# Two square roots on GpSimd by its power operation, and a convolution channel in three wide instructions

## The chip, the cores and the metric

One core of one Trainium2 chip. The metric is the device time of the whole kernel in microseconds, as the median of three runs.

## What is computed

A gated delta-rule attention layer and a mixture-of-experts layer, each added to its input and normalised. The change touches the attention only. Its reference, cut to what matters:

```python
def _short_conv(x, w):                       # 4 taps along time, one filter a channel, then silu
    xp = jnp.pad(x, ((0, 0), (cs - 1, 0), (0, 0)))
    return jax.nn.silu(sum((xp[:, i:i + t, :] * w[:, i] for i in range(cs))))
q = _short_conv(x @ Wq, conv_q)              # 8 heads of 128
k = _short_conv(x @ Wk, conv_k)              # 3 keys a token and head
v = _short_conv(x @ Wv, conv_v)              # 3 values a token and head
q = _l2norm(q) * d ** (-0.5)
k = _l2norm(k)                               # x * rsqrt(sum(x * x) + 1e-6)
def step(S, inp):                            # one token; S is 128x128 a head
    S = S * jnp.exp(gt)[..., None, None]
    for i in range(nh):
        kS = jnp.einsum('bhd,bhde->bhe', ki, S)
        S = S + bi[..., None, None] * (ki[..., None] * (vi - kS)[:, :, None, :])
    o = jnp.einsum('bhd,bhde->bhe', qt, S)
o = o * jax.lax.rsqrt(jnp.mean(o * o, -1, keepdims=True) + 1e-05) * rms_weight
o = o * jax.nn.silu(gate)
```

x is 2 x 2048 x 256.

## The kernel before

**Stages.** A setup splits the input and the weights into 16-bit pairs and makes small tables; then comes the recurrence over blocks, then the experts. The recurrence has 128 blocks: 8 stretches of 256 tokens for each of 16 pairs of batch and head. A block is cut into 8 chunks of 32 tokens, whose 96 keys and 32 queries make 128 rows; within a chunk the delta rule is a triangular system, inverted level by level (`level_x`, `level_t`, `level_tt`), and the state is carried from chunk to chunk (`from_state`, `solve`, `update`).

**Order.** The five engines run the same written-out pipeline. `run_bodies` calls each engine's `body(k)` 135 times; in body i, `k[s]` is the block i - s, so that up to 8 blocks are in work, and every engine does its instructions in the order of its `body`, each after its semaphore waits. `done(engine, count, key, n)` waits until the instruction `key` of block n has been done. The labels of stages differ between engines: GpSimd's `k[0]` is the block that ScalarE calls `k[1]`.

**The keys' norm.** GpSimd squares the keys (`square`, L1300), TensorE sums them (`norms`, L681), VectorE adds epsilon (`small_sq`, L1115: `k_sq`, 8 columns). ScalarE takes the root of `k_sq` as Exp(0.5 Ln(x)) in `key_ln` (L959) and `key_root` (L964); the result `sv` scales the values in VectorE's `keep_v` (L1160).

**The outputs' norm.** ScalarE sums the squares of the outputs (`square_outputs`), VectorE joins them with the queries' norms (`sum_squares`, L1200: `v_sum`, 2 columns), ScalarE takes the reciprocal root in `var_ln` (L1012) and `var_root` (L1018), and GpSimd scales the outputs by it (`scale_outputs`, L1340: `o_norm`). TensorE transposes `o_norm` (`turn_outputs`, L819), and VectorE multiplies by the gate (`gated_outputs`, L1208: `y_buf`), which SP stores. Ln and Exp lie in another table of ScalarE than Silu; it is loaded ahead of `var_ln` (L1063) and changed back at the next `silu` (L942). `exp_decay` (L954) lies between and needs it as well.

**The decay and the system.** TensorE makes the decays' exponents (`decays`, L717), ScalarE exponentiates them (`decay_tok`), GpSimd spreads them (`spread_decay`, L1291). TensorE makes the gram products (`gram`, L691), VectorE scales them by the decays (`system`, L1136: `n_t`), GpSimd subtracts the identity in place (`minus_one`, L1327), ScalarE rounds (`high`, L969), VectorE masks (`first_level`, L1145), TensorE transposes (`turn_first`, L725), and GpSimd makes the rest of the rounding (`low`, L1334: `n_low`).

**The convolution.** Seven channels of a block are convolved: six by ScalarE and VectorE from PSUM (L920, L1109), one, channel 6, by GpSimd from a copy in SBUF (`raw`, L928). GpSimd's is `tap(6, i, k)`: a scale by the filter's tap 0 (L1315), and for each of three more taps a scale into `tap_now` (L1319) and an add into `pool_acc` (L1321), on 256 columns each.

GpSimd's order in a body before:

```python
tap(6, 2, k[1]); scale_outputs(k[4]); piece(k[3]); tap(6, 3, k[1]); low(1, k[1])
square(k[0]); g_rows(k[0]); spread_decay(0, k[0]); spread_decay(1, k[0])
minus_one(0, k[0]); minus_one(1, k[0]); tap(6, 0, k[0]); tap(6, 1, k[0]); low(0, k[0]); square_q(k[1])
```

`piece` (L1352, L1354) splits a piece of the experts' weights, in 96 of the passes.

## Time and profile before

| | us |
|---|---|
| median of three runs | 4454.95 |
| the three runs | 4454.95, 4439.0, 4459.3 |
| span of the profiled execution | 4438.1 |
| TensorE matmul busy in it | 3992.3 (90%) |
| VectorE busy | 3484.2 (79%) |
| ScalarE busy | 3346.6 (75%) |
| GpSimd busy | 2391.0 (54%) |

In the rows PE is TensorE, DVE is VectorE, ACT is ScalarE, POOL is GpSimd and SPq is SyncE's DMA issue; L1340 is a line of the kernel. A wait's arrow points to what released it. Matmuls overlap and their ends are modelled. A share over the whole span mixes the setup, the recurrence and the experts, so waits and timelines of the recurrence are read beside it.

### The profile page before, as it was taken

The numbers are of one execution on the slowest core, as the hardware profiler recorded it, in microseconds if no ns is written. First come the engines' busy times: TensorE is split into PE (matmuls) and PEld (weight loads), VectorE is DVE, ScalarE is ACT, GpSimd is POOL, SyncE is SP. The second block draws the span as 40 slices with busy tenths as digits, with TensorE's granted clock in tenths as the row PEclk, the third lists the DMA queues.
The fourth block names the chain that finished last, engine by engine and source line by source line (L and its number), as shares of the span: only waits on it lengthen the run. The fifth ranks groups of instructions, "written<-read, shape, count | busy, mean of one in ns | idle before, by whom it ended". The sixth has DMA issues, their size and how long they took to land. (4 is left out here: it accounts for less than half of the span.)

```text
span 4438.1 us, 131600 instructions
## 1 busy us (share of the span) xinstructions
PE 3992.3 (90%) x47876; PEld 3643.0 (82%) x47876; DVE 3484.2 (79%) x9803; ACT 3346.6 (75%) x9029; POOL 2391.0 (54%) x2511
## 2 busy tenths in 40 slices
PE   1999999999999999999999999999999665899991
PEld 0899889899988888989889899998998454788881
DVE  6899999999998888999999999999998222444446
ACT  2888888888888888888888888888888211555551
POOL 3667666766765666676666666676667023000005
PEclk6999999999999999999999999999999887899996
DMA  6223223323333333332333333233332232666664
GB/s 255 59 83 104 77 77 90 100 73 83 104 83 72 83 85 83 86 90 85 82 90 87 85 89 86 85 92 85 83 86 80 87 117 89 221 228 232 232 235 129
DMA packets 307823, 485.07 MB, mean 109 GB/s; under 512 B 38784, under 2 KB 252800, under 8 KB 288384
## 3 DMA queue, kind: packets, MB, share of 16 engines
q1 hardware_dynamic: 290448, 449.65, 34.4%
q0 software_dynamic: 6144, 16.79, 1.2%
q10 hardware_dynamic: 10608, 10.23, 0.7%
q8 instruction: 404, 6.62, 0.6%
q14 instruction: 219, 1.79, 0.1%
HBM read 352.02 MB, written 107.75 MB: 104 GB/s over the span
## 5 line engine op out<-in xcount | busy, mean ns | idle before, releaser
L1109 DVE SCALAR_TENSOR_TENSOR conv_acc<-bank,conv_sb,conv_acc 128x256 f32<-128x256 f32 x2304 | 1090.0, 478 | 14.1 <-ACT conv_acc L920 4.7
L669 PE MATMUL bank<-x_cur,w_cur 128*128 128x259 f16 (+1 forms) x6144 | 856.1, 275 | 27.9 <-DVE v_rows L1097 24.9
L1168 DVE CAST_PREDICATED xs_lev<-mask_sb,bank 128x256 f16<-128x256 uint16 x1536 | 663.1, 432 | 96.8 <-PE bank L733 74.1
L980 ACT ACTIVATE inv<-bank 128x256 f16<-128x256 f32 x1536 | 606.5, 395 | 73.8 <-PE bank L745 53.0
L669 PEld LDWEIGHTS bank<-x_cur,w_cur 128*128 128x128 f16 (+1 forms) x6144 | 565.0, 98 | 92.9 <-DVE v_rows L1097 25.8
L1291 POOL TENSOR_TENSOR decay<-decay_tok,cst 128x512 f32<-128x512 f32 x256 | 320.1, 1272 | 489.2 <-ACT decay_tok L954 489.2
L989 ACT ACTIVATE invt<-bank 128x256 f16<-128x256 f32 x1280 | 509.0, 398 | 90.4 <-PE bank L757 71.6
L788 PE MATMUL bank<-state,kq_t 128*128 128x128 f32 x2048 | 447.9, 301 | 2.0 <-DVE state L1191 2.0
L733 PE MATMUL bank<-inv,n_high 128*128 128x64 f16 x6144 | 431.7, 192 | 3.8 <-issue 1.2
L796 PE MATMUL bank<-rhs,inv_t 128*128 128x128 f32 x2048 | 427.8, 301 | 3.1 <-DVE rhs L1184 3.1
L803 PE MATMUL bank<-w_sol,k_rows 128*128 128x128 f32 x2048 | 422.4, 298 | 2.1 <-ACT w_sol L999 1.9
L1327 POOL TENSOR_TENSOR n_t<-n_t,cst 128x512 f32<-128x512 f32 x256 | 326.5, 1275 | 172.8 <-DVE n_t L1136 172.7
L1300 POOL TENSOR_TENSOR squares<-kq_t 128x768 f32<-128x768 f32 x128 | 187.8, 1467 | 398.9 <-ACT kq_t L942 398.9
L920 ACT ACTIVATE conv_acc<-bank,conv_sb 128x256 f32<-128x256 f32 x768 | 364.2, 474 | 23.7 <-PE bank L669 4.6
L1191 DVE SCALAR_TENSOR_TENSOR state<-state,tables,bank 128x128 f32<-128x128 f32 x1024 | 339.8, 342 | 40.3 <-PE bank L803 21.2
L999 ACT ACTIVATE w_sol<-bank 128x128 f32<-128x128 f32 x1024 | 280.8, 275 | 111.9 <-PE bank L796 111.7
L745 PE MATMUL bank<-xs_lev,invt 128*128 128x64 f16 x5120 | 360.3, 192 | 2.2 <-ACT inv L980 0.4
L1319 POOL TENSOR_SCALAR tap_now<-raw_in,conv_sb 128x256 f32<-128x256 f32 x384 | 355.5, 926 | 12.3
L1184 DVE SCALAR_TENSOR_TENSOR rhs<-bank,tables,v_rows 128x128 f32<-128x128 f32 x1024 | 353.3, 345 | 10.5 <-PE bank L788 6.8
L757 PE MATMUL bank<-invt,xs_lev 128*128 128x64 f16 x5120 | 360.0, 192 | 1.4 <-issue 0.3
L1136 DVE SCALAR_TENSOR_TENSOR n_t<-bank,c_n,decay 128x128 f32<-128x128 f32 x1024 | 288.5, 345 | 85.6 <-PE bank L691 73.0
L1932 POOL DMA_INDIRECT y_one<-y_slots,y_row x32 | 30.3, 948 | 589.0 <-PEq L1925 579.6
(245 smaller groups left out, 11501.8 us busy)
## 6 DMA issues: line engine op xcount, KB each, us to landing
w_cur<-w_parts_scratch SPq DMA_DIRECT2D x128, 1024.0 KB, 10.5
ew<-e_parts_scratch SPq DMA_DIRECT2D x117, 896.0 KB, 6.2
x_cur<-x_parts_scratch SPq DMA_DIRECT2D x128, 259.0 KB, 7.2
x_slots<-no_rows SPq DMA_DIRECT2D x128, 256.0 KB, 10.4
e_parts_scratch<-e_pair SPq DMA_DIRECT2D x96, 224.0 KB, 7.4
o_rows<-w_sol SPq DMA_DIRECT2D x512, 32.0 KB, 4.0
y_scratch<-y_buf SPq DMA_DIRECT2D x128, 128.0 KB, 10.1
y_in<-y_scratch SPq DMA_DIRECT2D x32, 512.0 KB, 4.0
```

What stands on the lines that cost most here:

```text
L669: last = mm(bank[i % 2][:, 0:PW], w_cur[k.i % 2][:, wp, kt, c * P:(c + 1) * P].bitcast(BF16 if wp else F16), x_cur[k.i % 2][:, xp, kt, 0:P ...
L733: last = mm(packed(LEVX[:, u * HP:(u + 1) * HP], l), n_high[k.i % 2][g][:, u], half(inv[k.i % R_LEV][g][:, u], l, 0), start=True, stop=True)
L745: last = mm(packed(LEVT[:, u * HP:(u + 1) * HP], l), by[:, u], half(xs_lev[g][l - 1][:, u], l, 0), start=True, stop=True)
L757: last = mm(packed(LEVTT[:, u * HP:(u + 1) * HP], l), xs_lev[g][l - 1][:, u], half(invt[k.i % R_LEV][g][:, u], l, 1), start=True, stop=True)
L788: mm(chain(k), kq_t[k.i % R_KQ][:, c].rearrange("p a b -> p (a b)"), state[:, k.i % (B * H)], start=True, stop=True).then_inc(ks_made.sem, 1)
L796: mm(chain(k), inv_t[k.i % R_INV][:, c], rhs[k.i % 2][:], start=True, stop=True).then_inc(sol_made.sem, 1)
L803: mm(chain(k), k_rows[k.i % R_ROWS][:, c], w_sol[k.i % R_W][:, c], start=True, stop=True).then_inc(upd_made.sem, 1)
L920: a(conv_acc[turn_of(c, k, ON_DVE, 2)][:], bank[i % 2][:, 0:TB], ACT.Copy, scale=conv_sb[:, k.h, c, 0:1])\
L980: a(half(inv[k.i % R_LEV][g][:], l, 0), packed(halves(LEVT), l), ACT.Copy).then_inc(t_kept.sem, 1)
L989: a(half(dst, l, 1), packed(halves(LEVTT), l), ACT.Copy).then_inc(tt_kept.sem, 1)
L1109: v.scalar_tensor_tensor(acc, bank[at % 2][:, i:i + TB], conv_sb[:, k.h, c, i:i + 1], acc, ALU.mult, ALU.add).then_inc(tap_step.sem if i < ...
L1168: v.copy_predicated(half(xs_lev[g][l - 1][:], l, 0), half(mask4(l), l, 0).bitcast(U16), packed(halves(LEVX), l)).then_inc(x_kept.sem, 1)
```

## The change

ScalarE's four small activations for the roots go. GpSimd computes `sv` as `k_sq` to the power 0.5 in one instruction (`key_root`, between `spread_decay(1)` and `minus_one(0)`), and `rstd` in two (`var_root`, at the head of its body ahead of `scale_outputs`): an addition of epsilon and the power -0.5; a constant factor moves into `neg_rms`. Its convolution becomes `convolve`: one product of the four overlapping windows with the four taps (1024 columns), an add of the two halves (512 columns), and an add of what is left (256 columns), all behind `minus_one(1)`. To make room in SBUF, three constant tables that only the setup uses get a buffer of their own that is given up after the setup, so that the constants come by three DMAs in place of one. `sum_squares` now waits for the previous `rstd`, and `small_sq` for the `sv` of two blocks before. GpSimd's body after begins `var_root(k[4])`, `scale_outputs(k[4])`, `piece(k[3])`, `low(1, k[1])`, and the rest keeps its order but for `key_root(k[0])` and `convolve(6, k[0])`.

```diff
-C_ID, C_NEG, C_LATER, C_UPTO, C_ONES, C_SAME = range(6)
+C_ID, C_ONES, C_SAME = range(3)
+C_NEG, C_LATER, C_UPTO = range(3)
...
-        cst = sb("cst", [P, 6, P], F32)
+        cst = sb("cst", [P, 3, P], F32)
...
             scope = setup_scope
+            cst_once = sb("cst_once", [P, 3, P], F32)
...
                     sp.dma_start(wz_stage[:].rearrange("p a b -> p (a b)"), w_z).then_inc(z_in, 16)
-                    sp.dma_start(cst[:].rearrange("p a b -> p (a b)"), consts[:, 0:6 * P]).then_inc(consts_in, 16)
+                    sp.dma_start(cst[:, 0], consts[:, 0:P]).then_inc(consts_in, 16)
+                    sp.dma_start(cst_once[:].rearrange("p a b -> p (a b)"), consts[:, P:4 * P]).then_inc(consts_in, 16)
+                    sp.dma_start(cst[:, 1:3].rearrange("p a b -> p (a b)"), consts[:, 4 * P:6 * P]).then_inc(consts_in, 16)
...
                     nc.scalar.activation(alog_sb[:], alog_sb[:], ACT.Exp).then_inc(ac, 1)
-                    nc.scalar.activation(neg_rms[:], rms_raw[:], ACT.Copy, scale=-1.0)
+                    nc.scalar.activation(neg_rms[:], rms_raw[:], ACT.Copy, scale=-((EPS_RMS * DH) ** -0.5))
...
                                         ALU.subtract).then_inc(x_split_b, 1)
-                    dve.wait_ge(consts_in, 32)
+                    dve.wait_ge(consts_in, 64)
...
                     v.tensor_copy(identb[:], cst[:, C_ID])
-                    v.tensor_copy(negmask[:], cst[:, C_NEG, 0:CH])
-                    v.tensor_copy(laterb[:], cst[:, C_LATER])
-                    v.tensor_copy(uptob[:], cst[:, C_UPTO])
+                    v.tensor_copy(negmask[:], cst_once[:, C_NEG, 0:CH])
+                    v.tensor_copy(laterb[:], cst_once[:, C_LATER])
+                    v.tensor_copy(uptob[:], cst_once[:, C_UPTO])
...
             pool_acc = ring("pool_acc", R_PACC, [P, TB], F32)
-            tap_now = sb("tap_now", [P, TB], F32)
-            scaled_tap = sem("scaled_tap")
+            tap_prod = sb("tap_prod", [P, TAPS, TB], F32)
+            windows_scaled, taps_halved = sem("windows_scaled"), sem("taps_halved")
...
             c_k = ring("c_k", 2, [P, UN], F32)
-            ln_k = sb("ln_k", [P, UN], F32)
...
             v_sum = sb("v_sum", [P, 2], F32)
-            ln_v = sb("ln_v", [P, 2], F32)
             rstd = sb("rstd", [P, 2], F32)
+            v_eps = sb("v_eps", [P, 2], F32)
+            powers = sb("powers", [P, 2], F32)
             o_norm = sb("o_norm", [P, 2, P], F32)
-            eps_var = sb("eps_var", [P, 1], F32)
...
             squared, q_squared, g_made, scaled = map(sem, ("squared", "q_squared", "g_made", "scaled"))
-            gate_done, ln_made, norm_made, o_squared, var_ln_made, rstd_made = map(sem, (
-                "gate_done", "ln_made", "norm_made", "o_squared", "var_ln_made", "rstd_made"))
+            gate_done, norm_made, o_squared, var_made, rstd_made, powers_set = map(sem, (
+                "gate_done", "norm_made", "o_squared", "var_made", "rstd_made", "powers_set"))
...
                 (6, 1),))
-            pool_step = Count("pool_step", (
-                ((6, 2), 1), ((6, 0), 0), ((6, 1), 0)))
             pool_tapped = Count("pool_tapped", (
-                (6, 1),))
+                (6, 0),))
...
                     @at_stage
-                    def key_ln(k):
-                        done(act, rows_kept, "norms", k.n)
-                        a(ln_k[:], k_sq[k.i % 2][:], ACT.Ln).then_inc(ln_made, 1)
-
-                    @at_stage
-                    def key_root(k):
-                        act.wait_ge(ln_made, k.n + 1)
-                        a(sv[k.i % 2][:], ln_k[:], ACT.Exp, scale=0.5).then_inc(norm_made, 1)
-
-                    @at_stage
...
                         last.then_inc(o_squared, 1)
-
-                    @at_stage
-                    def var_ln(k):
-                        done(act, rows_kept, "queries", k.n)
-                        a(ln_v[:], v_sum[:], ACT.Ln, bias=eps_var[:, 0:1], scale=EPS_RMS * DH).then_inc(var_ln_made, 1)
-
-                    @at_stage
-                    def var_root(k):
-                        act.wait_ge(var_ln_made, k.n + 1)
-                        at_least(act, scaled, k.n)
-                        a(rstd[:], ln_v[:], ACT.Exp, scale=-0.5).then_inc(rstd_made, 1)
...
                         nc.scalar.preload_act_table_set("natural_log_exp_and_others")
-                        var_ln(k[4])
...
                         keep_t(5, 1, k[2])
-                        key_ln(k[1])
                         raw(6, k[1])
-                        key_root(k[1])
...
                         keep_w(6, k[3])
-                        var_root(k[4])
...
                     v.memset(state[:], 0.0)
-                    v.memset(eps_var[:], EPS_RMS * DH * EPS_K)
...
                         done(dve, rows_made, "norms", k.n)
+                        at_least(dve, norm_made, k.n - 1)
...
                         dve.wait_ge(o_squared, k.n + 1)
-                        at_least(dve, var_ln_made, k.n)
+                        at_least(dve, rstd_made, k.n)
...
                     @at_stage
-                    def tap(c, i, k):
-                        acc, src = pool_acc[turn_of(c, k, ON_POOL, R_PACC)][:], raw_in[turn_of(c, k, ON_POOL, R_RAW)][:, i:i + TB]
-                        if i == 0:
-                            done(pool, silu_done, *before(c, k, ON_POOL, R_PACC))
-                            done(pool, raw_kept, c, k.n)
-                            nc.gpsimd.tensor_scalar(acc, src, conv_sb[:, k.h, c, 0:1], None, ALU.mult).then_inc(pool_step.sem, 1)
-                            return
-                        at = TAPS * len(ON_POOL) * k.n + TAPS * ON_POOL.index(c) + i
-                        done(pool, pool_step, (c, i - 1), k.n)
-                        nc.gpsimd.tensor_scalar(tap_now[:], src, conv_sb[:, k.h, c, i:i + 1], None, ALU.mult).then_inc(scaled_tap, 1)
-                        pool.wait_ge(scaled_tap, at - at // TAPS)
-                        tt(acc, tap_now[:], acc, ALU.add).then_inc(pool_step.sem if i < TAPS - 1 else pool_tapped.sem, 1)
+                    def convolve(c, k):
+                        raw = raw_in[turn_of(c, k, ON_POOL, R_RAW)][:]
+                        windows = bass.AP(raw.tensor, raw.offset, [raw.ap[0], [1, TAPS], [1, TB]])
+                        done(pool, raw_kept, c, k.n)
+                        tt(tap_prod[:], windows, conv_sb[:, k.h, c, :, None].broadcast_to([P, TAPS, TB]), ALU.mult)\
+                            .then_inc(windows_scaled, 1)
+                        pool.wait_ge(windows_scaled, k.n + 1)
+                        tt(tap_prod[:, 0:2], tap_prod[:, 0:2], tap_prod[:, 2:4], ALU.add).then_inc(taps_halved, 1)
+                        done(pool, silu_done, *before(c, k, ON_POOL, R_PACC))
+                        pool.wait_ge(taps_halved, k.n + 1)
+                        tt(pool_acc[turn_of(c, k, ON_POOL, R_PACC)][:], tap_prod[:, 0], tap_prod[:, 1], ALU.add)\
+                            .then_inc(pool_tapped.sem, 1)
+
+                    @at_stage
+                    def key_root(k):
+                        done(pool, rows_kept, "norms", k.n)
+                        done(pool, rows_kept, ("values", 1), k.n - 2)
+                        tt(sv[k.i % 2][:], k_sq[k.i % 2][:], powers[:, 0:1].broadcast_to([P, UN]), ALU.pow).then_inc(norm_made, 1)
+
+                    @at_stage
+                    def var_root(k):
+                        done(pool, rows_kept, "queries", k.n)
+                        nc.gpsimd.tensor_scalar(v_eps[:], v_sum[:], EPS_K, None, ALU.add).then_inc(var_made, 1)
+                        pool.wait_ge(var_made, k.n + 1)
+                        tt(rstd[:], v_eps[:], powers[:, 1:2].broadcast_to([P, 2]), ALU.pow).then_inc(rstd_made, 1)
...
                     def body(k):
-                        tap(6, 2, k[1])
+                        var_root(k[4])
...
                         piece(k[3])
-                        tap(6, 3, k[1])
...
                         spread_decay(1, k[0])
+                        key_root(k[0])
...
                         minus_one(1, k[0])
-                        tap(6, 0, k[0])
-                        tap(6, 1, k[0])
+                        convolve(6, k[0])
...
+                    nc.gpsimd.memset(powers[:, 0:1], 0.5).then_inc(powers_set, 1)
+                    nc.gpsimd.memset(powers[:, 1:2], -0.5).then_inc(powers_set, 1)
+                    pool.wait_ge(powers_set, 2)
```

## Rows read from the trace of the kernel before

**Rows 1.** The page: busy time, share of the span and instructions of each engine.

```profile
PE 3992.3 (90%) x47876; PEld 3643.0 (82%) x47876; DVE 3484.2 (79%) x9803; ACT 3346.6 (75%) x9029; POOL 2391.0 (54%) x2511
```

**Rows 2.** Stretches: length, each engine's busy time (instructions), granted clock, DMA share, GB/s.

```profile
2000.00:3000.00 1000.00, 971.67 (x12685) 902.92 (x12685) 914.90 (x2635) 885.49 (x2475) 678.24 (x721) 1.00 0.31 88
```

**Rows 3.** Waits of TensorE over the recurrence: total us, times, longest.

```profile
PE bank L819 <- POOL o_norm L1340: 68.6, 124, 4.2
...
PE bank L699 <- DVE y_buf L1208: 21.0, 26, 2.2
```

**Rows 4.** Waits of GpSimd, VectorE, ScalarE over the recurrence, as rows 3.

```profile
POOL decay L1291 <- ACT decay_tok L954: 489.2, 128, 5.1
POOL squares L1300 <- ACT kq_t L942: 398.9, 128, 21.9
...
DVE y_buf L1208 <- DMA y_scratch<-y_buf: 45.7, 56, 2.6
...
ACT decay_tok L954 <- PE bank L717: 73.7, 128, 2.3
```

**Rows 5.** Timeline of GpSimd, one pass: start us, us, line, operation, idle before.

```profile
2007.96 1.27 POOL L1327 TENSOR_TENSOR n_t<-n_t,cst 128x512 f32<-128x512 f32 x1 [0.18 <-DVE n_t L1136]
2010.40 1.28 POOL L1327 TENSOR_TENSOR n_t<-n_t,cst 128x512 f32<-128x512 f32 x1 [1.17 <-DVE n_t L1136]
2011.65 0.93 POOL L1315 TENSOR_SCALAR pool_acc<-raw_in,conv_sb 128x256 f32<-128x256 f32 x1
2012.67 0.92 POOL L1319 TENSOR_SCALAR tap_now<-raw_in,conv_sb 128x256 f32<-128x256 f32 x1
...
2014.37 1.16 POOL L1334 TENSOR_TENSOR n_low<-n_t,n_high 128x512 bf16<-128x512 f32 x1
2015.48 0.61 POOL L1307 TENSOR_TENSOR q_sq<-kq_t 128x256 f32<-128x256 f32 x1
...
2017.08 0.73 POOL L1321 TENSOR_TENSOR pool_acc<-tap_now,pool_acc 128x256 f32<-128x256 f32 x1
2017.77 0.61 POOL L1340 TENSOR_TENSOR o_norm<-o_rows,rstd 128x256 f32<-128x256 f32 x1
...
2043.37 0.61 POOL L1340 TENSOR_TENSOR o_norm<-o_rows,rstd 128x256 f32<-128x256 f32 x1
```

**Rows 6.** Timelines of TensorE and VectorE, same pass, as rows 5.

```profile
2008.02 1.13 PE L691 MATMUL bank<-kq_t 128*128 128x128 f32 x8
...
2018.43 0.44 PE L819 MATMUL bank<-cst,o_norm 128*128 128x128 f32 x2 [0.53 <-POOL o_norm L1340]
...
2009.19 1.13 DVE L1136 SCALAR_TENSOR_TENSOR n_t<-bank,c_n,decay 128x128 f32<-128x128 f32 x4 [0.48 <-PE bank L691]
```

**Rows 7.** Groups of ScalarE by line: busy us, mean ns, idle before.

```profile
L1063 ACT ACT_TABLE_LOAD x133 | 170.6, 1283 | 22.6 <-DVE v_rows L1097 20.4
```

**Rows 8.** Groups of GpSimd by line and shape, columns as in rows 7.

```profile
L1300 POOL TENSOR_TENSOR squares<-kq_t 128x768 f32<-128x768 f32 x128 | 187.8, 1467 | 398.9 <-ACT kq_t L942 398.9
...
L1352 POOL CAST e_pair<-e_raw 128x448 f16<-128x448 f32 x96 | 53.6, 558 | 0.0
...
L1472 POOL CAST idx<-topi 128x8 f32<-128x8 uint32 x1 | 0.2, 191 | 0.1
...
L1469 POOL MEMSET eps_ln<- 128x1 f32 x1 | 0.1, 100 | 3.6 <-POOLq L585 3.6
```

**Rows 9.** VectorE's timeline, and lines L227, L1145: duration ns min/median/max, first and last start.

```profile
25.86 4.09 DVE L305 CAST ident<-cst 128x128 f16<-128x128 f32 x1
...
L227 POOL TENSOR_TENSOR w_pair<-w_stage,w_pair x8: 4055/4058/7137, 22.7 to 92.9; 128x2048 bf16<-128x2048 f32 x8
...
2013.30 0.28 DVE L1145 TENSOR_TENSOR first<-n_high,mask_sb 128x256 f16<-128x256 f16 x1
...
L1145 DVE TENSOR_TENSOR first<-n_high,mask_sb x256: 277/282/294, 131.2 to 3432.2; 128x256 f16<-128x256 f16 x128
```

**Rows 10.** Timeline of SyncE's DMA issues in the setup, columns as in rows 5.

```profile
1.64 0.43 SPq L200 DMA_DIRECT2D cst<-in_consts  x1
```

## The prediction

> **What bounds the kernel now.** The recurrence is 135 passes of one loop body, one in 25.6 us (from one `o_norm` to the next) [rows 5]; around it lie a setup and the experts, which the change hardly touches. I read the views in this order. The shares of the span put TensorE first with 90% [rows 1], and a stretch of 1000 us in the middle of the recurrence shows what that means there: TensorE is busy for 97% at the full granted clock (2.4 GHz), VectorE for 91%, ScalarE for 89%, GpSimd for 68% [rows 2]. So a faster engine other than TensorE is worth something only where TensorE waits for it. TensorE's waits name one such place that comes back in nearly every pass: the transposes of the scaled outputs (L819) wait for GpSimd's `o_norm`, 68.6 us in 124 times. The only other repeated one is 21.0 us in 26 times at L699, behind VectorE's `y_buf` [rows 3].
>
> Next, what makes `o_norm` late. GpSimd's long waits, for `decay_tok` and for the keys, come earlier in its round [rows 4], so its queue has caught up there, and what counts is the piece from the last wait to `o_norm`. In the timeline of one pass the second `n_t` starts at 2010.40 us after 1.17 us of idleness, and from its end on the queue runs without a pause, through five of the seven convolution instructions, `n_low` and `q_sq`, to `o_norm` at 2017.77 us [rows 5]. That `n_t` was released by VectorE's at 2009.19 us, and this by TensorE's gram product of 2008.02 us; TensorE has been waiting for 0.53 us when L819 starts at 2018.43 us [rows 6]. So a loop is closed each pass: gram product, `system(1)`, GpSimd's queue, `o_norm`, transposes. A tenth of a microsecond put into GpSimd's queue between `minus_one(1)` and `scale_outputs` is paid 128 times; a tenth taken out is gained 128 times, until the 68.6 us are used up.
>
> **The change, part by part.** *ScalarE loses four small activations a pass* (`var_ln`, `key_ln`, `key_root`, `var_root`). The table load ahead of them (1.28 us) stays, since `exp_decay` needs it [rows 7], and so does the one back at the next `silu`. TensorE has no repeated wait for ScalarE [rows 3], and `decay_tok`, for which GpSimd waits, itself waits for TensorE [rows 4]. I take nothing for it: TensorE's instructions cover it.
>
> *The root for the keys* goes between `spread_decay(1)` and `minus_one(0)`. Its input comes from `small_sq`, which VectorE does ahead of `system(0)`, so it waits for nothing. Behind it stand the first `n_t`, with 0.18 us of idleness ahead of it, and the second, with 1.17 us [rows 5]: up to 1.35 us never reach the second `n_t`. It delays the first, for which ScalarE (`high(0)`) and through it TensorE (`turn_first(0)`) wait; that lies between the gram product and L819, where a small delay only uses up part of TensorE's wait at L819. Nothing, then, while a power of 8 values is under 1.35 us; beyond that every further tenth is on the loop.
>
> *The convolution.* The starts give 2017.77 - 2011.65 = 6.12 us from the first scale to `o_norm`; 1.11 of it are `n_low`'s and 0.59 `q_sq`'s, so 4.42 are convolution [rows 5]. After, all of the convolution stands there: a product of 1024 columns, an add of 512, one of 256. For the product I take the line through `o_norm` (256 columns, 0.61 us, also with a broadcast operand) and `n_low` (512, 1.16 us), 2.14 ns a column: 1.16 + 512 x 0.00214 = 2.25 us [rows 5]. From above the line through the instructions that write in place, 0.73 and 1.27 us: 2.35. From below the squaring, 768 columns in 1.47 us [rows 8], 1.67 ns a column over the 0.61: 1.89. The add of 512 is in place like `n_t`, 1.27 us (from below 1.04, by the squaring's price); the last add lies between 0.61 and 0.73, and I take 0.67. A dependent instruction starts 0.09 us after the end of its forerunner (2011.65 + 0.93 to 2012.67), an independent one 0.03 us ahead of it [rows 5]. Sum 2.25 + 0.09 + 1.27 + 0.09 + 0.67 - 0.03 = 4.34 us against 4.42. The four slow scales go, but the last scale and add, which stood behind `o_norm`, have come ahead of it: a draw on the loop, whatever GpSimd's busy time falls by.
>
> *The root for the outputs* has the price. It comes directly ahead of `scale_outputs`: an addition on 2 columns, a gap, the power on 2 columns, a gap. Its input is ready (`sum_squares` ran in the pass before); the new wait of `sum_squares` for its result has most of a pass of slack. For the addition the nearest row is the cast of 8 columns, 0.19 us; from below the memset's 0.10. From above 0.71: a scale of 256 columns lasts 0.93 us [rows 5], and the two casts (448 columns 0.56, 8 columns 0.19) [rows 8] give 0.8 ns a column, so that up to 0.7 of the 0.93 may be fixed. The power shows nowhere in the trace. From below the memset's 0.10 us, from above, for the range, the 0.93 us of the dearest instruction of 256 columns; I take 0.30 us, near the small rows, for it has 2 columns only, and above the cast, for a power is more than a cast. With gaps 0.19 + 0.09 + 0.30 + 0.09 = 0.67 us.
>
> *Sum.* 4.34 + 1.11 + 0.59 + 0.67 = 6.71 us against 6.12: `o_norm` comes 0.59 us later, over 128 passes 75.5 us. Off it goes what other waits give back: where VectorE waits for the store of `y_buf` [rows 4], the store lands when it did, so each of the 26 waits at L699 (0.81 us in the mean) shrinks by up to 0.59 us, 15 us at most; as some are shorter I take 13. Net +62 us.
>
> *The rest.* Behind `o_norm` GpSimd has 1.7 us less to do, but what follows there is again a wait for ScalarE's keys [rows 4]: more idleness, nothing else. In the setup SP issues two more DMAs, each 0.43 us [rows 10], of the same bytes; between nothing and 0.9 us, and I take nothing, since VectorE and GpSimd are behind it with their wide subtractions.
>
> **A rule of the skill against the trace.** In the setup the two engines shut each other out: VectorE's cast of 128 columns took 4.09 us beside GpSimd's wide subtractions, and the longest of these 7.1 us where the median is 4.06 [rows 9]. In the recurrence VectorE's only long instruction with two operands in SBUF is `first_level` (L1145). The one at 2013.30 us ran inside a GpSimd scale (2012.67 to 2013.59, [rows 5]) and lasted 0.28 us; none of the 256 took over 0.294 [rows 9]. The Trainium skill (SBUF — State Buffer, section on the two separate sides) says that such a VectorE instruction and a GpSimd instruction that reads SBUF exclude each other for their whole length. The setup agrees, the recurrence does not. By that rule the wide product would hold `first_level(1)` back for some 0.6 us and GpSimd's add would then wait; this is case 5.
>
> **The cases.** (1) *Forecast*: the two operations ahead of `o_norm` are paid in each pass, 4517 us. For it: the wait at L819 comes in nearly all passes, so no slack takes them up. (2) *Faster, the other side*: the wide instructions run at the squaring's price. Then product 1.89, adds 1.04 and 0.61, roots and gaps 0.38 to 0.50: 5.77 to 5.9 us, `o_norm` 0.22 to 0.35 us sooner, 28 to 45 us less, 4410 to 4427. It decides from where product, adds, root and gaps together fall below 4.42 us (5.01 in my sum). Against it: the squaring reads one tensor twice, the product two. (3) *No change*: cheap small operations and a product near 2.1 us, 6.0 to 6.3 us in all, 4440 to 4475. (4) *The power is a long routine*: at 1.0 us for 2 columns 0.7 x 128 = 90 us above the forecast, 4607; at 3 us for each root, the keys' 1.65 beyond its cover, (2.7 + 1.65) x 128 = 557 above it, 5074. Nothing in the trace speaks for or against. (5) *Exclusion*: GpSimd's add waits some 0.25 us for a `first_level` that was itself held back (0.28 us from the product's end, less the 0.09 gap that is there anyway): 26 us more, 4543. (6) *It does not do what it says*: the keys' root isn't hidden even below 1.35 us, because `first_level(0)` comes late and holds VectorE's queue and so TensorE; at 0.2 us a pass this gives 4543 too.
>
> **How the numbers follow.** The profiled execution has a span of 4438.1 us; the three runs have 4439.0 to 4459.3 us, median 4454.95, 16.9 above the span. The sum is made against the span (4500 after), and the same 62 us stand on the median: 4517. Chances: case 1, with anything from 0.2 to 1.3 us more on the loop (4477 to 4600), 0.45; cases 5 and 6 together 0.07; case 4 0.13; case 3 0.20; case 2 0.15. With every unknown at its low end the piece is 5.77 us and the time 4410; with every one at its high end 2.35 + 0.09 + 1.27 + 0.09 + 0.73 - 0.03 + 1.70 + 0.71 + 0.09 + 0.93 + 0.09 = 8.02 us, 1.90 x 128 - 21 = +222, 4677. Eight times in ten: 4435 to 4605; that leaves out most of cases 2 and 4. A measurement can tell about 0.5%, 22 us, from no change: slower by more 0.65, within it 0.20, faster by more 0.15.
>
> **What would show it.** TensorE's wait for `o_norm` near 1.1 us a pass, some 140 us in all; the second `n_t` still with idleness ahead of it; a product of about 2.25 us and 6.7 us from its start to `o_norm`; as many table loads; TensorE's busy time unchanged. The prediction is wrong if the power on 2 columns is far from 0.3 us, if 1024 columns don't lie on the line of the rows, or if TensorE's next wait is elsewhere, at `turn_first(0)` above all.

## The result

The changed kernel takes 4545.26 us (median of 4 runs, 4537.4 to 4560.4) where the kernel before took 4446.98 (4 runs, 4436.5 to 4459.3): a ratio of 1.0232, with a 95% interval of 1.0203 to 1.0261. The forecast was slower by 62 us; it came to 98 us. The profiled execution has a span of 4548.3 us, 110.2 more than the kernel before's.

The page after, with the engines' busy times (compare [rows 1]):

```profile
PE 4044.3 (89%) x47876; PEld 3664.2 (81%) x47876; DVE 3568.1 (78%) x9802; ACT 3327.5 (73%) x8516; POOL 2467.1 (54%) x2385
```

The same stretch of 1000 us (columns as in [rows 2]):

```profile
2000.00:3000.00 1000.00, 951.41 (x12248) 875.96 (x12248) 907.65 (x2544) 849.85 (x2242) 680.14 (x659) 1.00 0.30 86
```

TensorE is busy for 951 us of 1000 where it was 972, at the same full clock: it waits more. Over the whole span its busy time did not stay as it was, as the prediction expected: it rose by 52 us for the same 47876 instructions, 39 of them in the recurrence. How much of that is only the way in which the ends are modelled isn't known. Where it waits, and who is behind that (the waits over the recurrence, compare [rows 3, 4]):

```profile
PE bank L726 <- DVE first L1121: 146.2, 129, 2.5
...
PE bank L820 <- POOL o_norm L1329: 3.7, 1, 3.7
...
DVE first L1121 <- ACT n_high L960: 128.0, 128, 1.1
...
ACT n_high L960 <- POOL n_t L1316: 155.4, 128, 3.2
```

The wait for `o_norm` (L820, L819 before) is gone but for one. In its place TensorE waits for `first_level` at `turn_first` (L726), 1.13 us in each pass, and the chain behind it reads downwards: `first_level` waits for ScalarE's `n_high`, that for GpSimd's `n_t`.

PEld is TensorE's loading of weights, which runs beside its matmuls and has waits of its own. One of them is new (kernel before, then changed kernel; the other half of each pair has no such repeated wait):

```profile
PEld bank L716 <- issue: 19.5, 112, 0.5
...
PEld bank L797 <- DVE rhs L1160: 25.5, 125, 0.2
```

L716 is the weight of `decays` and its wait has gone; L797 is a weight of the state's chain (`rhs`), and it now waits 0.20 us in each pass. Both come back below. One pass shows the main wait, first GpSimd (the timeline, columns as in [rows 5]):

```profile
2029.12 1.66 POOL L1303 TENSOR_TENSOR sv<-k_sq,powers 128x8 f32<-128x8 f32 x1
2030.74 2.49 POOL L1316 TENSOR_TENSOR n_t<-n_t,cst 128x512 f32<-128x512 f32 x2
2033.19 1.95 POOL L1290 TENSOR_TENSOR tap_prod<-raw_in,conv_sb 128x1024 f32<-128x1024 f32 x1
2035.22 1.27 POOL L1293 TENSOR_TENSOR tap_prod<-tap_prod 128x512 f32<-128x512 f32 x1
2036.64 0.73 POOL L1296 TENSOR_TENSOR pool_acc<-tap_prod 128x256 f32<-128x256 f32 x1
2037.33 1.15 POOL L1323 TENSOR_TENSOR n_low<-n_t,n_high 128x512 bf16<-128x512 f32 x1
2038.44 0.61 POOL L1283 TENSOR_TENSOR q_sq<-kq_t 128x256 f32<-128x256 f32 x1
2039.13 0.22 POOL L1308 TENSOR_SCALAR v_eps<-v_sum 128x2 f32<-128x2 f32 x1
2039.44 0.71 POOL L1310 TENSOR_TENSOR rstd<-v_eps,powers 128x2 f32<-128x2 f32 x1
2040.23 0.61 POOL L1329 TENSOR_TENSOR o_norm<-o_rows,rstd 128x256 f32<-128x256 f32 x1
```

And the other engines in the same pass:

```profile
2029.41 1.13 PE L692 MATMUL bank<-kq_t 128*128 128x128 f32 x8
...
2033.44 0.40 PE L726 MATMUL bank<-ident,first 128*128 128x128 f16 x4 [1.13 <-DVE first L1121]
...
2032.05 0.63 ACT L960 ACTIVATE n_high<-n_t 128x512 f16<-128x512 f32 x1 [1.19 <-POOL n_t L1316]
...
2032.71 0.68 DVE L1121 TENSOR_TENSOR first<-n_high,mask_sb 128x256 f16<-128x256 f16 x1 [1.01 <-ACT n_high L960]
...
2036.10 0.54 DVE L1121 TENSOR_TENSOR first<-n_high,mask_sb 128x256 f16<-128x256 f16 x1
...
2037.35 0.30 PEld L797 LDWEIGHTS bank<-rhs,inv_t 128*128 128x128 f32 x2 [0.20 <-DVE rhs L1160]
```

The keys' root (`sv`) takes 1.66 us, and both `n_t` follow it without a pause. Before, the first `n_t` started 0.06 us ahead of the gram product; now it starts 1.33 us behind it (2030.74 against 2029.41). `first_level` lasts 0.68 us where it had 0.28 [rows 9], and it ends 0.16 us after the second `n_t`. From the product's start to `o_norm` are 7.04 us (2033.19 to 2040.23); before, the piece had 6.12. The mean pass, from the first `o_norm` to the last of the 128, went from 25.75 us to 26.48: 92 of the 110 us. The recurrence begins 7 us later (first `o_norm` at 219.5 instead of 212.1), and what follows the last `o_norm` takes 966 us in place of 955. That last part holds the experts, whose code is the same in all versions; it took from 954 to 988 us in the profiled executions of this document, so its 11 us are no sign of the change.

The new kinds of instruction, grouped (columns as in [rows 8]):

```profile
L1290 POOL TENSOR_TENSOR tap_prod<-raw_in,conv_sb 128x1024 f32<-128x1024 f32 x128 | 249.9, 1952 | 0.0
L1303 POOL TENSOR_TENSOR sv<-k_sq,powers 128x8 f32<-128x8 f32 x128 | 212.4, 1659 | 0.0
...
L1310 POOL TENSOR_TENSOR rstd<-v_eps,powers 128x2 f32<-128x2 f32 x128 | 91.4, 714 | 10.7
```

### The profile page after: what moved, and what is told of

Read it like the earlier page. It is cut to its first block and busy times, and to the rows that moved or that the text cites. A ratio compares the mean times of both kernels' runs of the same rounds, so it can differ in the third digit from the quotient of the medians.

```text
span 4548.3 us, 131088 instructions
## 1 busy us (share of the span) xinstructions
PE 4044.3 (89%) x47876; PEld 3664.2 (81%) x47876; DVE 3568.1 (78%) x9802; ACT 3327.5 (73%) x8516; POOL 2467.1 (54%) x2385
## 5 line engine op out<-in xcount | busy, mean ns | idle before, releaser
L797 PE MATMUL bank<-rhs,inv_t 128*128 128x128 f32 x2048 | 438.5, 306 | 7.0 <-DVE rhs L1160 3.1
L734 PEld LDWEIGHTS bank<-inv,n_high 128*128 128x128 f16 x6144 | 325.2, 97 | 12.8 <-ACT inv L971 1.7
L797 PEld LDWEIGHTS bank<-rhs,inv_t 128*128 128x128 f32 x2048 | 299.0, 191 | 44.9 <-DVE rhs L1160 29.4
```

Source lines behind the costliest of these rows:

```text
L734: last = mm(packed(LEVX[:, u * HP:(u + 1) * HP], l), n_high[k.i % 2][g][:, u], half(inv[k.i % R_LEV][g][:, u], l, 0), start=True, stop=True)
L797: mm(chain(k), inv_t[k.i % R_INV][:, c], rhs[k.i % 2][:], start=True, stop=True).then_inc(sol_made.sem, 1)
```

## The experiments

Two causes stood to be told apart. Theory A: each pass has two gates in GpSimd's queue, the first `n_t` (delayed by the keys' root) and `o_norm` (delayed by the convolution and the outputs' root), and the higher of the two is paid, not their sum. Its rivals are that one part alone did it all, that the cost lies in what another engine lost or gained, or that the wide convolution is itself a loss. Ratios are to the kernel before on the same chip, with 95% intervals. The versions ran on four chips, on which the kernel before took 4438 to 4467 us, so versions are compared by their ratios and, in traces, by their mean pass, and not by their times in us.

### One part undone at a time

**The keys' root back on ScalarE**, all else as changed:

```diff
-                        key_root(k[0])          # GpSimd, ahead of minus_one(0)
+                        key_ln(k[1])            # ScalarE, as in the kernel before
                         raw(6, k[1])
+                        key_root(k[1])
```

> The changed kernel with one part undone: the keys' root goes back to ScalarE (Ln, then Exp at half scale), the outputs' root and the wide convolution stay on GpSimd. Theory A (two gates of nearly the same height: the keys' root holds minus_one(0) and so turn_first(0) back, and right beneath it the queue up to o_norm has become 7.04 us in place of 6.12): turn_first no longer waits, but TensorE now waits at the transposes of o_norm for 0.53 + 0.92 = 1.4 us a pass, so the time is only 5 to 20 us below the changed kernel, 4525 to 4540 us. Theory B (the keys' root is the whole cause, and the way to o_norm has slack): the time falls back to that of the kernel before, 4447 +- 15 us.

Measured 4502.3 us, 1.0131 (1.0097 to 1.0165). TensorE's waits from 500 to 3400 us (as for all waits from here on):

```profile
PE bank L823 <- POOL o_norm L1338: 139.6, 110, 1.6
```

The wait at `turn_first` is gone, and the one that the prediction named stands in its place: 1.27 us a pass where some 1.1 had been said, and 58 us in all where 62 had been. So the outputs' root and the convolution together cost about what was forecast (by errors that cancel, as is told further down), and the changed kernel hid this behind a higher gate. The time lies between the two numbers expected; the place is A's.

**The outputs' root back on ScalarE**, all else as changed:

```diff
-                        var_root(k[4])          # GpSimd, ahead of scale_outputs
+                        var_ln(k[4])            # ScalarE, behind the table load
...
+                        var_root(k[4])          # ScalarE, behind keep_w
```

> The changed kernel with the other part undone: the outputs' root goes back to ScalarE, the keys' root and the wide convolution stay on GpSimd. Theory A (the higher of two gates counts, not their sum): the queue up to o_norm is 1.1 us shorter, but the wait of 1.1 us at turn_first stays, and the time with it: 4530 to 4550 us. Theory C (the outputs' root ahead of o_norm is the cause, as the prediction had it): 0.22 + 0.71 + gaps, 1.1 us x 128, leaves, and the time falls to 4420 to 4460 us.

Measured 4571.2 us, 1.0282 (1.0245 to 1.0318).

```profile
PE bank L729 <- DVE first L1138: 120.7, 108, 1.1
```

The wait at `turn_first` stays, none for `o_norm` appears, and nothing is gained by taking the addition and the root (0.31 and 0.79 us, by starts) from ahead of `o_norm`: that gate isn't the higher one. It even takes somewhat more than the changed kernel (1.0232), though the intervals overlap; the mean pass is 26.62 us against 26.48. The traces show where: with `var_ln` back between the table load and `xs`, TensorE's weight load of `decays`, which writes into the bank that `xs` empties, waits again, 16.9 us in 98 times. This wait stands in every version that has the outputs' root on ScalarE and in none that has it on GpSimd.

**Both roots back**, so that the wide convolution alone is left:

```diff
-                        var_root(k[4])          # GpSimd
...
-                        key_root(k[0])          # GpSimd
                         minus_one(0, k[0])
                         minus_one(1, k[0])
                         convolve(6, k[0])
```

> One part of the change alone: the convolution in three wide instructions, both roots on ScalarE as before. From the changed kernel's durations the queue from minus_one(1) to o_norm is 7.04 - 1.10 = 5.94 us against 6.12 before. Theory A: TensorE's wait at the transposes shrinks by about 0.2 us a pass, if VectorE's first_level(1) isn't held back by the wide product for longer than that: 4415 to 4440 us, a little below the kernel before. Theory D (the wide instructions themselves cost, because VectorE's first_level with two SBUF operands waits for them): first_level lasts 0.5 us or more in both places, TensorE waits at turn_first, and the time is above the kernel before, 4460 to 4500 us.

Measured 4429.8 us, 0.9972 (0.9950 to 0.9993).

```profile
PE bank L706 <- DVE y_buf L1216: 31.9, 42, 2.6
```

The wide convolution is a small gain by itself, and the matmuls' wait for `o_norm` has gone (the weight load still waits for it, 25.7 us in 105 times), though the last scale and add have come ahead of it: the piece is 5.77 us in place of 6.12 (2006.26 to 2012.03). Where `o_norm` no longer holds a pass, the waits for `y_buf` grow (21.0 us in 26 times before, [rows 3]) and eat part of the gain. Measured from here, the outputs' root costs 1.0131 / 0.9972, 1.6%, the keys' root 3.1%, and both together 2.6%, which is the higher one's order of size and far from the sum of 4.7%. That is what A says.

**The old convolution with both roots on GpSimd**:

```diff
-                        convolve(6, k[0])
+                        tap(6, 0, k[0])
+                        tap(6, 1, k[0])
...
+                        tap(6, 2, k[1])         # ahead of var_root
...
+                        tap(6, 3, k[1])         # behind piece
```

> The changed kernel with the convolution as before (seven instructions of 256 columns, two of the taps' steps at their old places), both roots on GpSimd. Theory A: from minus_one(1) to o_norm 6.12 + 1.10 = 7.2 us and the keys' root as it was, so that the time is that of the changed kernel or up to 25 us more: 4545 to 4575 us. Theory D (the wide instructions cost by holding VectorE back): first_level returns to 0.28 us and the time falls by 40 us or more below the changed kernel, under 4510 us.

Measured 4619.2 us, 1.0389 (1.0350 to 1.0429), above what either expected.

```profile
PE bank L728 <- DVE first L1123: 184.1, 212, 1.2
```

Here TensorE waits for `first_level` about twice in a pass (212 times), also for the second one (timelines of GpSimd and VectorE):

```profile
2017.98 1.16 POOL L1325 TENSOR_TENSOR n_low<-n_t,n_high 128x512 bf16<-128x512 f32 x1
...
2018.12 1.17 DVE L1123 TENSOR_TENSOR first<-n_high,mask_sb 128x256 f16<-128x256 f16 x1
```

The second `first_level` starts just behind `n_low` and ends 0.15 us after it: it takes 1.17 us where 0.28 is usual, and `turn_first` then waits 0.60 us. The wide convolution, then, saves 1.5% (about 70 us) when the roots are there, and 0.3% when they are not. It is the part of the change that helps, and the forecast had it down as a small draw. But the wait of 0.60 us is about the whole difference between the mean passes (27.07 us here, 26.48 in the changed kernel): the 1.5% lies in that `n_low` no longer falls on `first_level`, and not in less work for GpSimd.

### The same work at another place

**The keys' root behind `low(1)`**, hence one body later, where GpSimd waits for ScalarE's keys anyway; its length is the same:

```diff
                         low(1, k[1])
+                        key_root(k[1])
                         square(k[0])
...
-                        key_root(k[0])
                         minus_one(0, k[0])
```

> The changed kernel with the keys' root moved in GpSimd's order, from ahead of minus_one(0) to behind low(1) of the next pass, where GpSimd has 4 us of idleness ahead of square. Everything stays on GpSimd, the power too. Theory A (its 1.66 us cost only by their place, because they hold minus_one(0) and first_level(0) back): the same as with that root on ScalarE, 4495 to 4515 us, with TensorE's wait at the transposes of o_norm 1.3 us a pass. Theory E (the power costs wherever it stands, for instance by keeping VectorE out of SBUF for 1.66 us): 4535 us or more.

Measured 4506.4 us, 1.0148 (1.0111 to 1.0185). `sv` still lasts 1.65 us.

```profile
PE bank L820 <- POOL o_norm L1329: 140.4, 110, 1.3
```

This is the picture of the version with the keys' root on ScalarE, at the same price. Not the length of the root by itself cost the time at the first gate, but its place; nor does it matter here whether ScalarE has the keys' root to do (a mean pass of 26.23 us in both versions).

**The convolution late too**, behind `scale_outputs`, so that both gates are freed:

```diff
                         scale_outputs(k[4])
+                        convolve(6, k[1])
                         piece(k[3])
                         low(1, k[1])
+                        key_root(k[1])
...
-                        convolve(6, k[0])
```

> As e5_keys_late, and the three wide instructions moved behind scale_outputs, so that between minus_one(1) and o_norm only low(0), square_q and the outputs' root stand, 2.8 us. Theory A (what counts is only what stands between minus_one and o_norm, not how long GpSimd works): TensorE waits neither at turn_first nor at the transposes; 0.53 us a pass less than the kernel before, 68 us, less some 15 us that come back as waits for the store of y_buf: 4375 to 4400 us. Theory F (ScalarE's silu of channel 6 or VectorE becomes the bound at once): 4420 us or more.

Measured 4405.0 us, 0.9912 (0.9889 to 0.9935): faster than both kernels, with all the changed kernel's instructions. The stretch:

```profile
2000.00:3000.00 1000.00, 984.06 (x12863) 916.83 (x12861) 923.11 (x2670) 881.08 (x2354) 713.20 (x693) 1.00 0.32 89
```

The only repeated wait of TensorE:

```profile
PE bank L700 <- DVE y_buf L1184: 40.5, 55, 2.5
```

GpSimd is busy for 713 us of 1000, where it had 678 before [rows 2] and 680 in the changed kernel, and TensorE waits for it no more. The time is a little above the range expected, by the waits for `y_buf`, which came back more than thought.

**Only the convolution late**, the keys' root where the change put it:

```diff
                         scale_outputs(k[4])
+                        convolve(6, k[1])
...
-                        convolve(6, k[0])
```

> The changed kernel with the wide convolution behind the scaling of the outputs, so that only the keys' root is left where the change put it. Theory A (two gates in each pass, the first n_t, delayed by the keys' root, and the wait for o_norm; the higher one is paid): the wait at turn_first stays, 0.7 to 1.1 us in nearly every pass, the wait for o_norm stays away, and since no product of the convolution runs beside first_level any more this drops back to 0.28 us. Against the version with both late (4405 us) the root alone costs 0.9 us x 128 = 115 us: 4500 to 4535 us. Rival B (what cost the time in the changed kernel is the convolution ahead of o_norm, and the keys' root is paid only together with it): 4405 to 4430 us, with no repeated wait at turn_first.

Measured 4537.7 us, 1.0157 (1.0139 to 1.0175).

```profile
PE bank L726 <- DVE first L1121: 124.0, 110, 1.1
```

The gate at `turn_first` stands alone and costs 1.6% over the kernel before, and 2.5% over the version with both late, some 109 us where A had 115. A's place and its size; B falls. One thing that A expected failed: `first_level` did not drop to 0.28 us. The pass shows why (timelines of GpSimd and VectorE):

```profile
2017.75 2.50 POOL L1316 TENSOR_TENSOR n_t<-n_t,cst 128x512 f32<-128x512 f32 x2
...
2019.72 0.68 DVE L1121 TENSOR_TENSOR first<-n_high,mask_sb 128x256 f16<-128x256 f16 x1 [1.02 <-ACT n_high L960]
```

The second `n_t` runs to 2020.25, and `first_level` ends at 2020.40. It isn't the wide product that holds `first_level(0)`, but the second `n_t`, and only because the root has pushed the two `n_t` together and `n_high` behind the start of the second. With the root elsewhere (`first_level` has a median of 0.28 us in the two versions before this one) there is nothing to hold it.

**The gates compared.** The mean passes of the traces test A's sum. With neither gate it is 25.51 us (both late), with `o_norm` alone 26.23 (keys' root on ScalarE, or late), with `turn_first` alone 26.29 (only the convolution late). If only the higher gate were paid, the changed kernel, which has both, would have 26.29; it has 26.48. The missing 0.19 us is the new wait at L797, 0.20 us a pass, which the version with only the convolution late doesn't have. The changed kernel's timeline shows its chain: the second `first_level` starts at 2036.10 beside GpSimd's add of 512 columns, ends 0.15 us after it and takes 0.54 us; in the version with the convolution late it takes 0.28 (at 2023.12). VectorE's queue, and in it `rhs`, is 0.26 us later for it, and the weight load waits for that. So of the 2.3%, some 0.5% by the mean pass, 0.75% by the ratios, are owed to the convolution standing beside the second `first_level` once the roots have delayed it; with the keys' root elsewhere the same convolution causes no such wait. The two gates don't add up, as A says, but this third one comes on top.

**Both roots on ScalarE, the convolution late**, to see what moving the roots is worth once nothing waits for GpSimd:

```diff
-                        key_root(k[1])          # GpSimd, from the version with both late
-                        var_root(k[4])
+                        var_ln(k[4])            # ScalarE, as in the kernel before
+                        key_ln(k[1])
+                        key_root(k[1])
+                        var_root(k[4])
```

> As e6_both_late, but both roots on ScalarE as in the kernel before: no power at all, three wide instructions behind scale_outputs. It tells what the roots on GpSimd are worth once they are off the way. Theory A: within 15 us of e6_both_late, ScalarE's four activations costing TensorE only some 0.1 us a pass at the decays: 4380 to 4410 us. Theory G (ScalarE's relief is worth its 0.7 us a pass): 40 us or more above e6_both_late.

Measured 4425.4 us, 0.9963 (0.9941 to 0.9985). Against 0.9912, the roots on GpSimd at harmless places are worth 0.5%, some 20 us: a small gain, where the forecast took nothing for ScalarE's relief. It is the weight load of `decays` again: it waits 18.4 us in 107 times here, and not at all in the version with both late. TensorE's matmuls [rows 3] don't show this wait.

### The prices

**The powers made products**, at their old places. This version leaves the two square roots out (it multiplies by the exponent), so that only the length of two instructions differs:

```diff
-                        tt(sv[k.i % 2][:], k_sq[k.i % 2][:], powers[:, 0:1].broadcast_to([P, UN]), ALU.pow)
+                        tt(sv[k.i % 2][:], k_sq[k.i % 2][:], powers[:, 0:1].broadcast_to([P, UN]), ALU.mult)
...
-                        tt(rstd[:], v_eps[:], powers[:, 1:2].broadcast_to([P, 2]), ALU.pow)
+                        tt(rstd[:], v_eps[:], powers[:, 1:2].broadcast_to([P, 2]), ALU.mult)
```

> The changed kernel with both powers replaced by products of the same operands at the same places: it leaves the roots out, so sv and rstd have other values, and its time is read for the price of the power alone. Theory A: the product on 8 columns takes about 0.2 us and fits under the idleness ahead of the second n_t, so turn_first no longer waits; the one on 2 columns takes about 0.2 in place of 0.71 us, the queue up to o_norm is 6.5 us against 6.12 before, and the time 4450 to 4475 us. This is the case that the prediction priced (0.30 us for the power). If small instructions cost as much as the power does, it is 4530 us or more.

Measured 4458.4 us, 1.0031 (1.0007 to 1.0055).

The two products, grouped:

```profile
L1303 POOL TENSOR_TENSOR sv<-k_sq,powers 128x8 f32<-128x8 f32 x111 | 22.6, 204 | 0.0
...
L1310 POOL TENSOR_TENSOR rstd<-v_eps,powers 128x2 f32<-128x2 f32 x111 | 21.6, 195 | 9.2
```

TensorE's wait:

```profile
PE bank L820 <- POOL o_norm L1329: 83.9, 111, 0.8
```

A keys' root of 0.20 us causes no wait at `turn_first`. So a short operation there is indeed hidden, as the prediction said; but 0.20 us is no more than the 0.18 us of idleness that the first `n_t` has ahead of it, so this doesn't bear out the bound of 1.35 us, and lengths between 0.20 and 1.66 us were not tried. And 1.0232 - 1.0031, 2% of the time, hangs on the length of the two powers alone.

**The prices by themselves**: the changed kernel with a prologue, in which GpSimd runs products, powers and additions of several sizes, and VectorE then a product of two tensors beside four kinds of GpSimd instruction.

```diff
+                    for op in (ALU.mult, ALU.pow):
+                        for n in (2, 8, 32, 64, 256):
+                            tt(tap_prod[:, 1, 0:n], tap_prod[:, 0, 0:n], powers[:, 0:1].broadcast_to([P, n]), op)
...
+                        v.tensor_tensor(o_norm[:], ident16[:, None, :].broadcast_to([P, 2, P]), mask_sb[:, 0:2], ALU.mult)
```

> The changed kernel with a prologue: before the recurrence's passes GpSimd multiplies, and then raises to a power, 2, 8, 32, 64 and 256 columns, adds a constant to 2, 64 and 256 columns by a scale-type instruction, and then VectorE runs one product of two tensors of 256 columns in SBUF four times, each beside another GpSimd instruction: a scale of 512 columns, a product of 512 columns of two tensors, a copy of 512 columns, a power of 16 columns. Prices: the power's line through the recurrence's two sizes (0.71 us for 2 columns, 1.66 us for 8) is 0.40 us and 0.157 us a column; by it 32 columns take 5.4 us, 64 take 10.4 us and 256 take 40.6 us. The rival, a routine that works on whole blocks of columns, gives steps: 32 columns well below 5 us. The products of 2 and 8 columns near 0.20 us, of 256 near 0.61 us; the scale-type addition on 2 columns 0.22 us and on 256 near 0.93 us. Exclusion: VectorE's product takes 0.28 us alone. Theory X (the kind of the GpSimd instruction decides): 0.28 us beside the scale, and about the GpSimd instruction's remaining length (0.6 to 1.2 us) beside the product of two tensors, and the power too, as it has two tensors as input. Theory Y (every GpSimd instruction that reads SBUF excludes it): held beside all four. Theory Z (only the length of the GpSimd instruction decides): beside the scale and the product alike 0.6 us or more, beside the power little.

The powers, and the product of 256 columns, grouped by form:

```profile
L1380 POOL TENSOR_TENSOR tap_prod<-tap_prod,powers 128x256 f32<-128x256 f32 x1 | 0.7, 694 | 0.1
...
L1380 POOL TENSOR_TENSOR tap_prod<-tap_prod,powers 128x256 f32<-128x256 f32 x1 | 41.1, 41127 | 0.1
L1380 POOL TENSOR_TENSOR tap_prod<-tap_prod,powers 128x64 f32<-128x64 f32 x1 | 10.5, 10522 | 0.1
L1380 POOL TENSOR_TENSOR tap_prod<-tap_prod,powers 128x32 f32<-128x32 f32 x1 | 5.4, 5416 | 0.1
L1380 POOL TENSOR_TENSOR tap_prod<-tap_prod,powers 128x8 f32<-128x8 f32 x1 | 1.8, 1793 | 0.1
```

The first line is the product, the others powers. From 64 to 256 columns a power takes (41.127 - 10.522) / 192 = 0.159 us a column, and the line is straight, so the rival of blocks falls; a product of 256 takes 0.69 us. For the same 256 columns a power costs 59 times as much.

What GpSimd does to VectorE (timelines of both, each probe of VectorE beside the GpSimd instruction above it):

```profile
166.39 1.58 POOL L1391 TENSOR_SCALAR tap_prod<-tap_prod,conv_sb 128x512 f32<-128x512 f32 x1
...
166.69 0.67 DVE L1082 TENSOR_TENSOR o_norm<-ident,mask_sb 128x256 f32<-128x256 f16 x1
...
168.09 1.04 POOL L1393 TENSOR_TENSOR tap_prod<-tap_prod 128x512 f32<-128x512 f32 x1
...
168.31 1.09 DVE L1082 TENSOR_TENSOR o_norm<-ident,mask_sb 128x256 f32<-128x256 f16 x1
...
169.72 0.61 POOL L1395 COPY tap_prod<-tap_prod 128x512 f32<-128x512 f32 x1
...
169.94 0.67 DVE L1082 TENSOR_TENSOR o_norm<-ident,mask_sb 128x256 f32<-128x256 f16 x1
...
170.91 2.93 POOL L1397 TENSOR_TENSOR tap_prod<-tap_prod,powers 128x16 f32<-128x16 f32 x1
...
171.14 0.42 DVE L1082 TENSOR_TENSOR o_norm<-ident,mask_sb 128x256 f32<-128x256 f16 x1
```

Beside a product VectorE's ended 0.27 us after GpSimd's (169.40 against 169.13): held for its whole length. Beside a copy of 512 columns it was the same (ended 0.28 us after). Beside the scale (a TENSOR_SCALAR) it ended 0.61 us ahead of GpSimd's end, and beside the power 2.28 us ahead: no exclusion for the length of either. X is right on the product and in that the scale doesn't hold the probe to its end, and wrong on the power; Y and Z fall. How long the probe takes alone was not measured. It is at most the 0.42 us that it took beside the power, so beside the scale at least 0.25 us of the 0.67 were a delay of some kind; X's 0.28 us wasn't met.

### The next limit

**Three buffers for `y_buf`** in the version with both late, since its only repeated wait was there:

```diff
-            y_buf = ring("y_buf", 2, [P, TB], F32)
+            y_buf = ring("y_buf", 3, [P, TB], F32)
...
-                        at_least(dve, stored[k.i % 2], 16 * (k.turn(2)))
+                        at_least(dve, stored[k.i % 3], 16 * (k.turn(3)))
```

> The version with the keys' root and the convolution both late (4405 us, 0.991 of the kernel before), with three buffers for y_buf in place of two, so that VectorE no longer waits for the store of the block two passes ago. In that version VectorE waits 97.8 us for those stores in 91 times and TensorE 42.4 us for y_buf in 56 times. Theory A (TensorE's wait for y_buf is real time that the third buffer gives back): 42 us of TensorE's waits go, 4365 to 4380 us, 0.982 to 0.986 of the kernel before. Rival H (the wait is only where the slack of a pass ends, and another wait takes its place, for o_norm or turn_first, or TensorE's own work bounds the pass): 4395 to 4410 us, with a new repeated wait elsewhere.

Measured 4361.0 us, 0.9752 (0.9733 to 0.9772), the fastest of all.

```profile
2000.00:3000.00 1000.00, 992.11 (x13070) 930.85 (x13069) 939.35 (x2711) 894.68 (x2393) 718.70 (x695) 1.00 0.32 88
```

TensorE is busy for 992 us of 1000, and none of its waits in the recurrence comes to 4 us in all. The gain over the two-buffer version is 1.6%, more than the 42 us of TensorE's waits that A counted: the mean pass fell from 25.51 to 24.92 us, 76 us in all. Why it is more than the waits isn't shown. After the recurrence this version took 988 us against 957 (from the last `o_norm` to the end), and the experts start at a lower granted clock (0.82 in the 200 us from 26 us after the last `o_norm` on, against 0.91 with two buffers). But the two ran on different chips, and on this one the version with only the convolution late, which has two buffers, took 982 us there as well; so no part of the 31 us can be put down to the third buffer.

**Three buffers in the kernel before**, and nothing else (the diff is the same):

> The kernel before, with three buffers for y_buf and nothing else. The version with both placements late and three buffers took 0.975 of the kernel before, with both late and two buffers 0.991; here the third buffer stands alone. Theory A (two gates in a pass, of which the higher is paid: in the kernel before it is the wait for o_norm, 68.6 us in 124 times, and the wait for y_buf, 21.0 us, only adds where o_norm was early): the wait for y_buf goes, that for o_norm stays in nearly every pass and grows by some of it, to 70 to 90 us; at most the 21 us are gained, 0.995 to 1.000 of the kernel before. Rival I (the third buffer is worth its 70 us wherever it stands, and the placements had little to do with it): 0.980 to 0.988.

Measured 4406.8 us, 0.9932 (0.9910 to 0.9955).

```profile
PE bank L820 <- POOL o_norm L1341: 57.4, 110, 0.6
```

Neither number was met, though the interval touches A's range. The wait for `o_norm` stays as it was (56.9 us in 109 times before, over the same stretch) and didn't grow to A's 70 to 90, and 0.7% is gained, more than TensorE's 21 us of waits for `y_buf` [rows 3]. The buffer alone is worth 0.7%, not I's 1.6%; the late placements give the other 1.8% (0.9752 / 0.9932). Why freeing a wait of 21 us gives some 30 isn't settled: VectorE, held at `y_buf` for 45.7 us [rows 4], is late for its other work as well, which would fit and was not shown.

## Why the prediction was right, and where it was wrong

**The gate, the step that failed.** The direction and the range held, the mechanism did not. The prediction took the keys' root as hidden while under 1.35 us, and said of the first `n_t` that a small delay there only uses up TensorE's wait at L819. The first half was right for the second `n_t`: before, it started 2.38 us after the gram product (2008.02 to 2010.40), after 2.55 (the two end at 2033.23, and one lasts 1.27 us). With 1.66 us against 1.35, 0.31 us was due and 0.17 came. The other half was wrong. The first `n_t` has only 0.18 us ahead of it and started 1.39 us later against the gram product, and behind it stands a chain of its own, `n_high`, `first_level`, `turn_first`. In this pass TensorE starts `turn_first` 4.03 us after the gram product (2033.44 against 2029.41). In the kernel before it was 2.75, without a wait (its timeline, [rows 6] has the gram product at 2008.02):

```profile
2010.77 0.39 PE L725 MATMUL bank<-ident,first 128*128 128x128 f16 x4
```

That is 1.28 us, more than the 0.53 us of wait at L819 that it could use up. The text knew of it: it is case 6, with 0.2 us a pass, and the last point of what would make it wrong. But case 6 shared a chance of 0.07 with case 5, its price was a sixth of the wait that came (1.13 us a pass), and the sum had nothing for it; it would have been seen by adding 1.66 - 0.18 to the first `n_t` and asking what TensorE has left to do before `turn_first`.

**Idleness in a queue is owned by the instruction that it stands ahead of.** The 1.17 us ahead of the second `n_t` could not cover work put ahead of the first one.

**The price of the power.** Taken as 0.30 us on 2 columns, measured 0.71; the range given, 0.10 to 0.93, held it. For 8 columns no value was taken, only the bound of 1.35, and 1.66 us was above it. Price goes with the columns, 0.159 us each; the prediction's guess that few columns make it cheap was right in direction and took too small a slope. The truth lies between the forecast and case 4 (1.0 us for 2 columns, 3 us for a long root of the keys); the roots' length alone is worth 2%.

**The piece to `o_norm`.** Predicted 6.71 us, measured 7.04. By starts, in us: the product 2.03 in place of 2.34 (it lasts 1.95 and not 2.25, near the squaring's price per column, which the prediction took as its lower end); the first add 1.42 for 1.36; the last 0.69 for 0.64; `n_low` 1.11 for 1.11; `q_sq` 0.69 for 0.59; the addition 0.31 for 0.28; the power 0.79 for 0.39. The sum of the differences is +0.33, of which the power alone is +0.40.

**The waits.** The forecast had 140 us of waits for `o_norm`. The changed kernel shows one such wait, and the two versions with the keys' root taken away show 139.6 and 140.4 us. The forecast mechanism is real, but it was not the one that set the time in the changed kernel, and that its size came out (58 and 66 us for 62) is luck. The piece grew by 0.92 us and not by 0.59; at the forecast's rule, each tenth paid in each pass, this is 118 us, or 97 with all the 21 us at L699 given back. Paid were 0.48 us a pass (25.75 to 26.23). Some 0.15 to 0.17 of the rest is the wait of `decays`' weight load that went with the outputs' root, which the sum took as nothing; so the power priced too low and ScalarE's relief left out cancelled each other. That the direction of the whole held, and that 98 us lie in the range around 62, is owed to the gate at `turn_first` being of the same sign.

**The signs.** Of the five that the prediction named, one came: as many table loads (132 and 129 where 133 and 129 had been, in ScalarE's two lines). The product took 1.95 us for about 2.25, the second `n_t` has no idleness ahead of it, TensorE's 1.13 us a pass of waiting are at `turn_first`, and its busy time rose by 52 us.

**The convolution.** Called a draw; it is a gain, 0.3% alone and 1.5% with the roots (there by where `n_low` falls). The forecast compared lengths from the first scale to `o_norm` and had 4.34 us against 4.42. By starts the three instructions had 2.03 + 1.42 + 0.69 = 4.14 us in the changed kernel; the line for the product was too dear by 0.31.

**ScalarE's relief, taken as nothing.** It is worth 0.5%, and the traces show it only for the outputs' root: without `var_ln` behind the table load, `xs` and with it the weight load of `decays` come earlier (19.5 us of waits before, none after). The prediction looked for waits of TensorE on ScalarE among the matmuls alone [rows 3]; this one stands among the weight loads. The relief shows beside a gate of GpSimd too (26.48 us a pass in the changed kernel, 26.62 with the outputs' root back). The keys' root gives none, as far as two versions tell that both wait for `o_norm` (26.23 us a pass with it on either engine).

**Exclusion.** Case 5 had it at the wide product, with GpSimd's add waiting behind it, 26 us (its own terms, 0.28 less 0.09 us, give 24). That isn't what came: the add starts 0.08 us after the product's end, as it does without a wait. The second `first_level` is held by that add (0.54 us for 0.28), and what pays is TensorE's weight load behind VectorE's `rhs`, 25.5 us in all: about the size of case 5 by another path. And another pair has it: `first_level(0)` is held by the second `n_t`, 0.68 us for 0.28, and the 0.40 us lies on the gate at `turn_first`, some 51 us over 128 passes if all of it is paid. By the section of the Trainium skill that the prediction cited (SBUF — State Buffer, on the two separate sides) such a pair excludes each other; the product of two tensors agrees (1.09 us, ended 0.27 us behind GpSimd's), the scale and the power do not (ended 0.61 and 2.28 us ahead). The row on which the prediction doubted it showed `first_level` inside a scale, and so spoke for scales only. Nor does the setup's row speak for such a pair, as the prediction has it: its VectorE instruction is a cast, with one operand [rows 9]. The change itself put products in the scales' place.

## What to carry to other kernels

An operation that is put into an engine's queue is costed against each instruction behind it up to the next long wait, and for each of these the chain that hangs on it is followed to the engine that bounds the kernel; idleness covers only what stands between it and the instruction that waits, and of several gates the highest is paid, so that a gate can look free until the higher one is taken away. Waits of the weight loads are read beside those of the matmuls: two terms of this case, 0.2 us a pass each, stood only there. Here the same instructions cost 2.3% at one place and gained 0.9% at another, where the queue waited for other work anyway. An operation of unknown kind should be measured at two sizes before its place is chosen, for its price may be per column.
